# Scores of the causal and cross attentions over two row groups of 64 channels, one bank each

## What is computed

```python
# layer 0, causal: weights are squared softplus, not a softmax
scores = einsum('bhqd,bhkd->bhqk', q, k) * 8 ** -0.5
p = softplus(scores) ** 2 * causal
out = einsum('bhqk,bhkd->bhqd', p / (p.sum(-1) + 1e-9), v)
# layers 0 and 1, cross: q from x, k and v from the context, rotary embedding on q and k
attn = softmax(q_rot @ k_rot.T * 8 ** -0.5 (+ key mask in layer 0))
out = attn @ v
```

## Time and profile before

| what | us |
|---|---|
| median of the runs | 781.32 |
| lowest and highest of 3 runs | 778.82, 783.33 |
| span of the profiled execution, its own time | 788.8 |
| PE busy | 633.0 (80%) |
| PEld busy | 513.6 (65%) |
| DVE busy | 505.0 (64%) |
| ACT busy | 381.3 (48%) |
| POOL busy | 230.7 (29%) |
| the scores matmuls of L330, PE busy (a and l tiles) | 84.2 and 42.3 |

### The profile page before, as it was taken

The page is one execution under the profiler, slowest core; times in us unless marked ns, Lnnn a source line. Parts: engine busy times, 40 slices in busy tenths (PEclk is TensorE's granted clock), DMA queues, the critical chain, the costliest instruction groups (busy, mean ns, idle before and its releaser), DMA issues. The chain is left out here.

```text
span 788.8 us, 12952 instructions
## 1 busy us (share of the span) xinstructions
PE 633.0 (80%) x3779; PEld 513.6 (65%) x3786; DVE 505.0 (64%) x1221; ACT 381.3 (48%) x966; POOL 230.7 (29%) x254
## 2 busy tenths in 40 slices
PE   4898885999999968699889999979999988781006
PEld 3777774777777756467668888868777776430006
DVE  3788983656675745744544444447677676469886
ACT  3778883445444532133235444435455463484615
POOL 3555552323222211356500000014334331005220
PEclk9899996989997958899979999989899797695558
DMA  5400000001000000000000000001010000000001
GB/s 158 160 11 10 10 13 14 21 21 28 24 20 17 0 1 1 0 1 2 1 11 7 11 10 7 17 14 27 20 26 21 19 17 0 1 0 0 0 0 54
DMA packets 30649, 15.29 MB, mean 19 GB/s; under 512 B 18513, under 2 KB 29841, under 8 KB 30610
## 3 DMA queue, kind: packets, MB, share of 16 engines
q1 hardware_dynamic: 30610, 14.82, 6.7%
HBM read 10.09 MB, written 1.05 MB: 14 GB/s over the span
## 5 line engine op out<-in xcount | busy, mean ns | idle before, releaser
L330 PE MATMUL bank<-a_mov,a_stat 128*128 128x256 f32 x256 | 84.2, 459 | 12.0 <-issue 10.2
L514 DVE TENSOR_REDUCE rowmax<-bank 128x8 f32<-128x512 f32 x64 | 44.2, 691 | 62.2 <-PE bank L330 61.4
L330 PEld LDWEIGHTS bank<-a_mov,a_stat 128*128 128x128 f32 x256 | 50.6, 219 | 28.7 <-issue 23.0
L1213 POOL TENSOR_TENSOR e_hid<-e_gated,e_relu 128x512 f32<-128x512 f32 x32 | 40.6, 1270 | 57.0 <-DVE e_gated L1328 56.8
L1088 PEld LDWEIGHTS bank<-body_sb,e_hid 128*128 128x128 f32 x288 | 37.7, 196 | 22.0 <-issue 13.9
L139 POOL TENSOR_TENSOR xb<-X,made_bias 128x128 f32<-128x128 f32 x32 | 14.6, 457 | 117.2 <-DVE r L149 103.8
L1190 ACT ACTIVATE e_relu<-bank 128x512 f32<-128x512 f32 x36 | 21.5, 598 | 54.2 <-PE bank L1066 45.1
L1328 DVE TENSOR_TENSOR e_gated<-e_relu,bank 128x512 f32<-128x512 f32 x32 | 21.9, 686 | 36.6 <-PE bank L1076 22.5
L252 POOL TENSOR_TENSOR a_stat<-qk,head_sb 128x512 f32<-128x512 f32 x32 | 33.3, 1041 | 37.5 <-ACT qk L405 36.3
L330 PE MATMUL bank<-l_mov,l_stat 128*128 128x256 f32 x128 | 42.3, 462 | 2.2 <-POOL l_mov L252 2.0
L469 ACT ACTIVATE oT<-bank 64x64 f32<-64x64 f32 x192 | 41.7, 217 | 4.1 <-PE bank L375 2.0
(11 more groups left out here) (262 smaller groups left out, 1716.3 us busy)
## 6 DMA issues: line engine op xcount, KB each, us to landing
kvT<-in_ctxT SPq DMA_DIRECT2D x64, 64.0 KB, 2.1
xs<-X SPq DMA_DIRECT2D x56, 64.0 KB, 1.9
body_sb<-in_body SPq DMA_DIRECT2D x2, 950.0 KB, 5.1
body_sb<-in_body SPq DMA_DIRECT2D x2, 949.5 KB, 5.2
out<-X SPq DMA_DIRECT2D x4, 256.0 KB, 2.3
X<-in_x SPq DMA_DIRECT2D x1, 896.0 KB, 6.0
mid_sb<-in_mid SPq DMA_DIRECT2D x1, 448.0 KB, 3.6
head_sb<-in_head SPq DMA_DIRECT2D x1, 422.0 KB, 3.2
```

Source lines behind the costliest of these rows:

```text
L330: mm = nc.tensor.matmul(psS[b][:, 256 * half:256 * half + 256], m.stat[:, par, b, 2 * half:2 * half + 2, :], m.mov[:, par, b, :, :], start ...
L514: nc.vector.tensor_reduce(m.rowmax[:, b, :], psS[b][:, :].rearrange("p (x k) -> p x k", k=T), AX.X, ALU.max).then_inc(s[f"max_done{b}"].se ...
L1213: nc.gpsimd.tensor_tensor(m.hid[:, n % DEEP, :], a, m.relu[:, n % DEEP, :], ALU.mult).then_inc(s["hid_ready"], 1)
```

## The change

The channels are split into two halves of 64, g = 0 and 1, that is i in {0, 1} and i in {2, 3}. `stat` now holds two copies per sequence and `mov` four, and a scores matmul contracts over the 64 channels of one half only: rows 0 to 63 for g = 0, rows 64 to 127 for g = 1, with the same 128 columns of `stat` and 256 of `mov` as before. The half g writes the bank `psS[g]`, with both sequences in it. The two calls per tile become one, with 4 matmuls in the order (b 0, g 0), (b 0, g 1), (b 1, g 0), (b 1, g 1). It stands behind turn in both lists; in the causal attention `scores0` leaves its old place at the end of the slot before. The mask matmuls of both banks come first, over 128 rows of which all but one are zero. The later steps with suffix 0 and 1 now go by half and not by sequence; the lists of DVE, ACT and POOL keep their order. The columns of the masks in the constants change accordingly, and DVE clears the larger mask tile once at the start.

```diff
@@ -243,7 +243,7 @@
 
-        def mask_operand(t, par, out, which, mask, done):
+        def mask_operand(t, par, out, n, which, mask, done):
             if causal:
@@ -251,21 +251,20 @@
                 out[:, par, :, :, :],
-                m.qk[:, par, which, :].rearrange("p (b k) -> p b k", b=SB).unsqueeze(2).broadcast_to([P, SB, 4, T]),
-                mask.unsqueeze(1).unsqueeze(3).broadcast_to([P, SB, 4, T]), ALU.mult).then_inc(s[done].sem, 1)
+                m.qk[:, par, which, :].rearrange("p (b k) -> p b k", b=SB).unsqueeze(2).broadcast_to([P, SB, n, T]),
+                mask.unsqueeze(1).unsqueeze(3).broadcast_to([P, SB, n, T]), ALU.mult).then_inc(s[done].sem, 1)
 
...
         def stationary(t, par):
-            mask_operand(t, par, m.stat, 1 if causal else 0, m.mask_ca if causal else m.mask_ac, "stat_ready")
+            mask_operand(t, par, m.stat, 2, 1 if causal else 0, m.mask_a if causal else m.mask_c, "stat_ready")
 
         def moving(t, par):
-            mask_operand(t, par, m.mov, 0 if causal else 1, m.mask_i, "mov_ready")
+            mask_operand(t, par, m.mov, 4, 0 if causal else 1, m.mask_jc if causal else m.mask_ja, "mov_ready")
 
...
             wait(pool, s["o_psum1"], t - 1)
-            soft = m.soft[:, 1, :].rearrange("p (c i q) -> p c i q", c=2, i=NI)
-            nc.gpsimd.tensor_tensor(m.prob[:, par, 1, :, :, :].rearrange("p i c q -> p c i q"), soft, soft,
+            nc.gpsimd.tensor_tensor(m.prob[:, par, 1, :, :, :].rearrange("p n c q -> p (n c q)"), m.soft[:, 1, :], m.soft[:, 1, :],
                                     ALU.mult).then_inc(s["prob_ready1"].sem, 1)
@@ -316,33 +315,32 @@
 
-        def scores(t, par, b):
+        def scores(t, par):
 
...
             wait(pe, s["mov_ready"], t + 1)
-            wait(pe, s[f"shifted{b}"], t)
+            for g in range(2):
+                wait(pe, s[f"shifted{g}"], t)
             if masked:
-                nc.tensor.matmul(psS[b][:, :], m.ones_bf[0:1, :],
-                                 w.mask_row[0:1, bass.ds(t * P + b * T, T)].unsqueeze(1).broadcast_to([1, 8, T]),
-                                 start=True, stop=False, skip_group_check=True)
-            for half in range(2):
-                mm = nc.tensor.matmul(psS[b][:, 256 * half:256 * half + 256], m.stat[:, par, b, 2 * half:2 * half + 2, :],
-                                      m.mov[:, par, b, :, :], start=not masked, stop=True, skip_group_check=masked)
-            mm.then_inc(s[f"s_psum{b}"].sem, 1)
-
-        def scores0(t, par):
-            scores(t, par, 0)
-
-        def scores1(t, par):
-            scores(t, par, 1)
+                for g in range(2):
+                    nc.tensor.matmul(psS[g][:, :], m.ones_bf[:, :],
+                                     m.mask_row[:, bass.ds(t * P, P)].rearrange("p (b k) -> p b k", b=SB).unsqueeze(2)
+                                     .broadcast_to([P, SB, 4, T]), start=True, stop=False, skip_group_check=True)
+            for b in range(SB):
+                for g in range(2):
+                    rows = slice(64 * g, 64 * g + 64)
+                    mm = nc.tensor.matmul(psS[g][:, 256 * b:256 * b + 256], m.stat[rows, par, b, :, :],
+                                          m.mov[rows, par, b, :, :], start=not masked, stop=True, skip_group_check=masked)
+                    if b == SB - 1:
+                        mm.then_inc(s[f"s_psum{g}"].sem, 1)
 
...
             wait(pe, s[f"exp_done{b}"], t + 1)
-            for i in range(NI):
-                mm = nc.tensor.transpose(psT[b][:, i * P:(i + 1) * P], m.prob[:, par, b, i, :, :], m.ident)
+            for n in range(4):
+                mm = nc.tensor.transpose(psT[b][:, n * P:(n + 1) * P], m.prob[:, par, b, n, :, :], m.ident)
             mm.then_inc(s[f"pT_psum{b}"].sem, 1)
@@ -357,10 +355,11 @@
             wait(pe, s[f"prob_ready{b}" if causal else f"pT_ready{b}"], t + 1)
-            for i in range(NI):
-                lhsT = m.prob[:, par, b, i, :, :] if causal else m.probT[:, b, i, :]
-                at = 36 * (NI * b + i)
-                mm = nc.tensor.matmul(psO[:, at:at + 36], lhsT, m.vals[:, par, b, i, :, :, :], start=True, stop=True)
+            for n in range(4):
+                seq, i = n // 2, 2 * b + n % 2
+                lhsT = m.prob[:, par, b, n, :, :] if causal else m.probT[:, b, n, :]
+                at = 36 * (NI * seq + i)
+                mm = nc.tensor.matmul(psO[:, at:at + 36], lhsT, m.vals[:, par, seq, i, :, :, :], start=True, stop=True)
             mm.then_inc(s[f"o_psum{b}"].sem, 1)
@@ -381,10 +380,10 @@
             if causal:
-                run(turn, 0), run(scores1, 1), run(project_outputs, 3), run(project, 0), run(outputs0, 2)
-                run(outputs1, 2), run(values, 0), run(scores0, 0), run(turn_outputs, 2)
+                run(turn, 0), run(scores, 1), run(project_outputs, 3), run(project, 0), run(outputs0, 2)
+                run(outputs1, 2), run(values, 0), run(turn_outputs, 2)
             else:
-                run(turn, 0), run(scores0, 1), run(outputs1, 2), run(project, 0), run(scores1, 1), run(turn_probs0, 1)
+                run(turn, 0), run(scores, 1), run(outputs1, 2), run(project, 0), run(turn_probs0, 1)
                 run(values, 0), run(turn_outputs, 2), run(outputs0, 1), run(project_outputs, 2), run(turn_probs1, 1)
@@ -418,7 +417,7 @@
         def exponential(t, par, b):
-            sc = m.prob[:, par, b, :, :, :].rearrange("p i a k -> p (i a k)")
+            sc = m.prob[:, par, b, :, :, :].rearrange("p n a k -> p (n a k)")
             if causal:
@@ -445,13 +444,13 @@
             wait(act, s["o_psum0"], t - 1)
-            nc.scalar.activation(m.prob[:, par, 0, :, :, :].rearrange("p i c q -> p c i q"),
-                                 m.soft[:, 0, :].rearrange("p (c i q) -> p c i q", c=2, i=NI), ACT.Square).then_inc(s["prob_ready0"].sem, 1)
+            nc.scalar.activation(m.prob[:, par, 0, :, :, :].rearrange("p n c q -> p (n c q)"), m.soft[:, 0, :],
+                                 ACT.Square).then_inc(s["prob_ready0"].sem, 1)
 
...
             wait(act, s[f"o_psum{b}"], t)
-            nc.scalar.activation(m.probT[:, b, :, :].rearrange("p i q -> p (i q)"), psT[b][:, :],
+            nc.scalar.activation(m.probT[:, b, :, :].rearrange("p n q -> p (n q)"), psT[b][:, :],
                                  ACT.Copy).then_inc(s[f"pT_ready{b}"].sem, 1)
@@ -518,10 +517,9 @@
             wait(dve, s[f"pT_psum{b}"], t - 1)
-            nc.vector.tensor_tensor(m.prob[:, par, b, :, :, :].rearrange("p i a k -> p a i k"),
-                                    psS[b][:, :].rearrange("p (a i k) -> p a i k", a=2, i=NI),
-                                    m.rowmax[:, b, :].rearrange("p (a i) -> p a i", a=2).unsqueeze(3)
-                                    .broadcast_to([P, 2, NI, T]),
+            nc.vector.tensor_tensor(m.prob[:, par, b, :, :, :].rearrange("p n a k -> p (n a) k"),
+                                    psS[b][:, :].rearrange("p (x k) -> p x k", k=T),
+                                    m.rowmax[:, b, :].unsqueeze(2).broadcast_to([P, 8, T]),
                                     ALU.subtract).then_inc(s[f"shifted{b}"].sem, 1)
@@ -942,10 +940,10 @@
     m.rope = sb("rope", [P, 2, 2, 2, P])
-    m.stat = sb("stat", [P, 2, SB, 4, T])
-    m.mov = sb("mov", [P, 2, SB, NI, T])
-    m.prob = sb("prob", [P, 2, SB, NI, 2, T])
-    m.probT = sb("probT", [P, SB, NI, P])
+    m.stat = sb("stat", [P, 2, SB, 2, T])
+    m.mov = sb("mov", [P, 2, SB, 4, T])
+    m.prob = sb("prob", [P, 2, 2, 4, 2, T])
+    m.probT = sb("probT", [P, 2, 4, P])
     m.soft = sb("soft", [P, SB, 512])
@@ -1686,11 +1684,12 @@
 
-        m.ident, m.mask_ac, m.mask_ca, m.mask_i, m.causal = h("ident"), h("mask_ac"), h("mask_ca"), h("mask_i"), h("causal")
+        m.ident, m.causal = h("ident"), h("causal")
+        m.mask_a, m.mask_c, m.mask_ja, m.mask_jc = h("mask_a"), h("mask_c"), h("mask_ja"), h("mask_jc")
         m.cos, m.sin = mi("cos"), mi("sin")
         m.mask_u8 = sb("mask_u8", [1, NSEQ * T], U8)
-        m.mask_row = sb("mask_row", [1, NSEQ * T], BF16)
-        m.ones_bf = sb("ones_bf", [1, P], BF16)
+        m.mask_row = sb("mask_row", [P, NSEQ * T], BF16)
+        m.ones_bf = sb("ones_bf", [P, P], BF16)
         m.one = sb("one", [P, 1])
@@ -1767,12 +1766,13 @@
                 nc.vector.memset(m.cq[:, :, :], 0.0)
+                nc.vector.memset(m.mask_row[:, :], 0.0)
                 nc.vector.memset(m.f[LC + LR:, :, :], 0.0).then_inc(s["memset"], 1)
...
                 dve.wait_ge(m.load["mask"], 16)
-                nc.vector.tensor_scalar(m.mask_row[:, :], m.mask_u8[:, :], 1.0, BIG, ALU.subtract, ALU.mult)
+                nc.vector.tensor_scalar(m.mask_row[0:1, :], m.mask_u8[:, :], 1.0, BIG, ALU.subtract, ALU.mult)
 
@@ -1826,9 +1826,12 @@
     p = np.arange(P)
-    c["mask_ac"] = (p[:, None] // HD % 4 == np.arange(4)).astype(np.float32)
-    c["mask_ca"] = np.ascontiguousarray(c["mask_ac"][:, [0, 2, 1, 3]])
```

(9 more changed lines are left out.)

## The result

| kernel | median us (lowest to highest, runs) | ratio to before, 95% interval | granted clock, profiled run |
|---|---|---|---|
| before | 782.33 (778.82 to 789.48, 4) | | 0.869 |
| changed | 829.84 (825.93 to 832.99, 4) | 1.0617 [1.0558, 1.0676] | 0.810 |

A forecast was written before the change was run, and what follows sets the result against it. No engine was taken as full; loops of waits close each slot, in the crosses through DVE's list. Causal +4, L0 +6.5, L1 +7, lower clock -3 gave +14.5, say +15 us: 796, range 786 to 810.

The forecast's parts named there:

- +14.5 us: Whole kernel: sum of the causal, L0, L1 and lower-clock terms, on the profiled span of 788.8 us.
- A load starts when the pass before it starts and never earlier, and the two passes of one group can't overlap.: Scores call: in-order overlap assumed for its eight passes; the call lasts 1.43 us, bank 0 is 0.22 later.
- rival (b): Scores call: both groups of a sequence start together, 4 x 0.22 us; -10 us in all, 771; chance 0.10.
- L1 +0.6 per slot: Biased cross attention of the second layer: later projection delays the rotation; 12 slots at the upper clock, +7 us.
- L0 +0.5: Masked cross attention: later projection delays the rotation by 0.67, less 0.2 slack; 13 slots, +6.5 us.
- 0.11 charged, bounds 0 and 0.23: Behind the scores call: going from 64 rows back to 128 costs one unhidden load, in us.
- +0.22 charged: L0: both mask matmuls now stand ahead of the scores, adding a 512-column pass; between 0.22 and 0.32 us.
- Causal +4: Causal stage: second clamp may wait behind a_mov, delaying denominators 0.74 us per slot; ends 0 and +9.6, +4 us taken.
- rival (c): Scores call: no overlap, bank 0 +0.44, PE +0.88, clamp falls into a_mov for sure; +33 us, 814; chance 0.14.
- Stretches at the lower clock: -3: Lower-clock stretches: the call costs 2.86 us for 3.44, 0.35 saved per slot, some 10 slots, -3 us.
- Rival (d), the clock: Longer slots give PE less to do, the clock falls more often: 40 us more low clock, +16, 812; chance 0.10.
- (a): Scores call: full pipelining of the groups, loads go ahead of waiting passes, 1.10 us; sum -2.5, 779; chance 0.24.

The follow-up runs named there:

- e5: Changed kernel plus a filler of four matmuls nobody reads, behind the values in the causal attention; 808.72 us, ratio 1.0304.
- e1: Changed kernel with each scores matmul over all 128 rows, which makes the scores different; 850.72 us, ratio 1.0849.
- e2: Kernel before with only the order changed: both scores calls of a tile together behind turn; 861.49 us, ratio 1.1003.
- f1: Changed kernel; in the crosses bank 1's maximum and subtraction moved ahead of the rotation, its exponential behind bank 0's; 845.68 us, ratio 1.0793.
- e3: Changed kernel with its four scores matmuls issued once more ahead of the mask, to be written over; 860.85 us, ratio 1.095.
- e7: Changed kernel plus unread filler matmuls in the causal attention behind the values and in the crosses behind the projection; 787.95 us, ratio 1.0054.

## Why the prediction was wrong

*Forecast, 796 and slower*: the sign was right, the size and most of the mechanism were not. The sign was in part luck: most of the +14.5 us came from an overlap taken as too poor, and what made the kernel slower had been counted as a gain.

1. **"A load starts when the pass before it starts and never earlier, and the two passes of one group can't overlap."** The first step that failed. The call lasts 1.07 us to the next group and not 1.43, the groups' passes start 7 ns apart in the L0 slot and 7 to 36 in the L1 slot, and bank 0 isn't later. That is rival (b)'s condition, to which I gave 0.10. The Trainium skill ("TensorE: Matmul & The Clock Gate", part 3) draws tiles of different row groups as starting some 4 ns apart and running together; the trace agrees in the main, with 7 ns and up to 36, also for these two-pass fp32 matmuls. I had cited the part on loads and overlooked that one.
2. **L1 +0.6 per slot and L0 +0.5.** The rotation came 0.13 and 0.23 us later, the slots 8.2 and 8.5 to 8.7 against 7.8 to 8.1 and 8.4 to 8.5. The projection keeps the rotation waiting for 0.17 us in L1, and that is all. With these the two terms would be some +1.5 to +3.5 us each and not +7 and +6.5. The parts of these terms that don't come from the overlap held: the call takes 1.07 us to the next group in L1 and 1.06 in L0, where four passes took 0.94 and 0.97, so beside the overlap the row groups cost 0.09 to 0.13 (0.11 charged, bounds 0 and 0.23), and in L0 the two mask matmuls take 0.53 to the scores where one took some 0.3 (+0.22 charged).
3. **Causal +4, the clamp against a_mov.** The race was read rightly. It is decided by less than 0.1 us, and at the upper clock it goes either way: in e5's alternating slots the clamp takes 0.43 and the slot 6.64, or 1.22 to 1.27 and the slot 7.1. That is +0.25 a slot against the earlier trace rows, some 3 us in 13 slots if none of it is the filler's, and near the +4 that had been taken as a middle value. a_stat takes 0.61 and not 0.70. In the changed kernel itself, mostly at the lower clock, the clamp starts 0.2 us ahead of a_mov from the slot at 60.5 us on and takes 0.5 to 0.6. In e1, with rival (c)'s passes one after the other, it falls behind a_mov in some slots and not "for sure".
4. **"Stretches at the lower clock: -3."** The step that missed the result. I priced what the shorter passes save in such stretches and held the stretches' share fixed. The time at the lower clock rose by over 100 us, and that is nearly the whole loss: L1's slots with 6.8 us of it take 10.7 us, 2.7 more than those without, 0.4 per us; the causal slot at the lower clock throughout takes 2.5 us more in 9.1, 0.27 per us. 121 us at 0.27 to 0.4 is 33 to 48, and the measured difference is 47 in the medians, 35 in the profiled spans. The kernel before shows the same price from run to run: a line through 28 of its runs, 776.5 to 789.6 us at clocks of 0.894 to 0.869, gives 0.28 us per us at the lower clock.
5. **Rival (d), the clock**, 812 at 0.10, named the mechanism: it was mis-sized (40 us more at the lower clock, where the runs had 106 to 121) and placed in slots that become longer. Its larger part came in the causal stage, through TensorE's own saving and not through longer slots: e2, whose causal slots had no pass taken out, kept the clock. "Against: the idle that is added is short" was the wrong argument: the earlier trace rows showed all three stages already between the two levels, which was the warning. Rival (b) was right on the passes, and (a) came near the call's length (1.10) by another mechanism; both were wrong on the time, since they too held the clock fixed. (c) is what e2 and e1 show for passes one after the other: its +0.95 and +0.75 us a slot are about there at the upper clock (e2's first L1 slot takes 8.83, its L0 slots 9.3, for 7.9 and 8.4), and both kernels are dearer than 814 because of the clock.

**What is shown and what isn't.** Shown: work for TensorE in the emptied places returns the clock and 42 of 47 us, and the same work in the kernel before raises the clock and doesn't help. Shown: in the causal stage the order alone leaves the clock alone. Not separated: how much TensorE has to run, and where in the slot. e1 has the amount back at the slot's head with a causal clock of 0.83, e5 has it in TensorE's wait with 0.95. Argued only: how the order lowers the clock in the crosses. e1, e2 and f1 lengthen the waits that TensorE has within a slot, and have clocks below before's in both crosses, while e3's L0 keeps 0.91; and no run lengthens a wait without moving something else. How the 4 us left in e7 split between the row groups' 0.1 us in each call and the rest isn't measured either.

## What to carry over

Where the granted clock already stands between its two levels, TensorE work that nobody waits for isn't free to remove: price a saving there at both signs, by the cost of a slot at either level. Look at how the clock stands in each stage before counting a shorter matmul as a gain. And read idle time ahead of a step in slots at both clock levels before moving work into it.

## What the runs showed of the hardware

- Two row groups of 64 run fp32 matmuls side by side for all their passes: the two starts of a pair are 7 to 36 ns apart in most calls (up to 73 where the clock changes within one), and the pairs follow at 0.216 us at the upper clock (the second comes 0.32 behind the first) and 0.427 at the lower, whether issued alternately or half by half.
- Going back from 64 rows to 128 costs some 0.1 us: the next group starts 0.30 behind the last pair (in L0 the fourth pair starts at 201.36 and the outputs' first matmul at 201.67), where a pass of this size takes 0.216. The Trainium skill ("TensorEngine Tiling (Array Packing)", key properties) has it that switching the mode drains the TensorE; the trace is in line with that and makes it cheap: an estimate from these starts is 48 calls of 0.1, at most 5 us.
- VectorE's clamp and GpSimd's masked copy hold one another up, and which starts first decides: in e5 the clamp takes 0.43 us and a_mov 1.30 when the clamp starts 0.02 us ahead; the clamp takes 1.22 to 1.27 and a_mov 1.04 when it starts 0.05 to 0.11 us behind, and it then ends 0.28 behind a_mov.
- Until its first record (15.1 us before, 30.1 after) the clock reads 1.00 in the window view while the matmuls run at the lower level; the distance between starts, 0.213 against 0.112 us for 128 columns, tells.
